# Reordering the expert stage of a two-layer transformer kernel

## The reference, cut to what matters

```python
xn = _layernorm(x, axis=-1)
x = x + _L1_attn_ref(xn, ...) + _L1_ffn_ref(xn, ...)

# _L1_attn_ref
scores = jnp.einsum('bhqd,bhkd->bhqk', q, k) * scale
scores = jnp.where(causal, scores, jnp.float32(-jnp.inf))
probs = jax.nn.softmax(scores, axis=-1)
attn = jnp.einsum('bhqk,bhkd->bhqd', probs, v)
out = attn @ weight_proj.T

# _L1_ffn_ref, E = 32, K = 4, CAP = 32
probs = jax.nn.softmax(x @ Wr, axis=-1)
topw, topi = jax.lax.top_k(probs, K)
topw = topw / jnp.sum(topw, axis=-1, keepdims=True)
shared = silu(x @ Wsg) * (x @ Wsu) @ Wsd
shared = shared * jax.nn.sigmoid(x @ Wse)
pos = (jnp.cumsum(oh, axis=0) * oh).sum(-1) - 1        # oh: one-hot of the chosen experts
xe = jnp.zeros((E, CAP, h), x.dtype).at[sel, posc].add(x[tok] * valid[:, None])
g = silu(jnp.einsum('ech,ehf->ecf', xe, Wg))
u = jnp.einsum('ech,ehf->ecf', xe, Wu)
ye = jnp.einsum('ecf,efh->ech', g * u, Wd)
out = shared.at[tok].add(ye[sel, posc] * (w * valid)[:, None])
```

## Time and profile before

| | |
|---|---|
| median of 3 runs | 461.1 us (460.25 to 461.37) |
| profiled execution | 461.18 us, span 459.2 us |
| TensorE matmul busy | 427.9 us (93%) |
| VectorE busy | 311.3 us (68%) |
| ScalarE busy | 245.5 us (53%) |
| GpSimd busy | 165.7 us (36%) |
| TensorE, 372.21 to 438.87 us | 54.23 us busy of 66.66, mean granted clock 0.92 |

### The profile page before, as it was taken

The page is one execution under the profiler, slowest core; times in us unless marked ns, Lnnn a source line. Parts: engine busy times, 40 slices in busy tenths (PEclk is TensorE's granted clock), DMA queues, the critical chain, the costliest instruction groups (busy, mean ns, idle before and its releaser), DMA issues.

```text
span 459.2 us, 8817 instructions
## 1 busy us (share of the span) xinstructions
PE 427.9 (93%) x3054; PEld 380.9 (83%) x3054; DVE 311.3 (68%) x901; ACT 245.5 (53%) x669; POOL 165.7 (36%) x293
## 2 busy tenths in 40 slices
PE   2999999999999999999999999999998889785997
PEld 1788888899999999999999999999976655564787
DVE  5645576678787878787877766586779636948142
ACT  3464561786868787868676873332254225502020
POOL 3050001545454555555555301021650061897000
PEclk9999999999999999999999999999999999988899
DMA  6820011401010101010000000001999039950002
GB/s 192 214 74 2 1 46 47 156 29 47 2 46 1 47 3 46 1 49 1 0 2 2 0 1 25 13 11 30 340 312 301 11 117 300 284 149 0 1 12 80
DMA packets 41978, 34.45 MB, mean 75 GB/s; under 512 B 6688, under 2 KB 40144, under 8 KB 41936
## 3 DMA queue, kind: packets, MB, share of 16 engines
q1 hardware_dynamic: 41552, 32.85, 25.1%
q0 software_dynamic: 384, 1.05, 0.7%
HBM read 31.80 MB, written 2.10 MB: 74 GB/s over the span
## 4 chain that ended last, share of the span: by engine, by line
PE 87%; DVE 8%; ACT 2%; issue 2%; DMA 1%; POOL 0%; DVEq 0%
PE bank L910 21%; PE bank L912 21%; PE bank L911 21%; PE bank L1068 4%; PE bank L1080 3%; PE bank L1059 3%; DVE GT L1752 2%; PE bank L1309 2%; PE bank L1310 2%; PE bank L1285 2%; PE bank L1110 2%; PE bank L1267 1%; DVE ACTl L1810 1%; DVE OS L1756 1%; PE bank L1298 1%
## 5 line engine op out<-in xcount | busy, mean ns | idle before, releaser
L573 POOL TENSOR_TENSOR arena<-arena,rinv 128x384 f32<-128x384 f32 x64 | 52.9, 827 | 82.2 <-DVE rinv L1550 82.2
L910 PE MATMUL bank<-XTl,WA 128*128 128x512 f32 x128 | 54.4, 425 | 2.6 <-POOL WA L540 1.7
L912 PE MATMUL bank<-XTh,WA 128*128 128x512 f32 x128 | 51.4, 401 | 0.0
L911 PE MATMUL bank<-XTh,WA 128*128 128x512 f32 x128 | 51.3, 401 | 0.0
L739 ACT ACTIVATE PT<-bank 128x256 fp32r<-128x256 f32 x64 | 24.4, 381 | 34.2 <-PE bank L1068 34.2
L1554 DVE TENSOR_TENSOR PT<-bank,PT 128x256 fp32r<-128x256 f32 x64 | 27.2, 425 | 19.7 <-ACT arena L740 19.7
L910 PE MATMUL bank<-WA,XTh 128*128 128x256 f32 x128 | 38.4, 300 | 0.6 <-DVE K L1525 0.6
L911 PE MATMUL bank<-WA,XTl 128*128 128x256 f32 x128 | 35.8, 279 | 0.0
L564 POOL CAST Q<-arena 128x128 fp32r<-128x128 f32 x64 | 18.6, 290 | 47.7 <-PE bank L912 47.6
L912 PE MATMUL bank<-WA,XTh 128*128 128x256 f32 x128 | 35.7, 279 | 0.0
L1542 DVE CUSTOM_DVE_ANT_0 arena<-bank,posm 128x128 f32<-128x128 f32 x64 | 18.1, 283 | 20.9 <-PE bank L912 20.9
(11 more groups left out here) (326 smaller groups left out, 1453.8 us busy)
## 6 DMA issues: line engine op xcount, KB each, us to landing
arena<-in_L_ffn_Wg SPq DMA_DIRECT2D x6, 704.0 KB, 7.8
arena<-in_L_ffn_Wu SPq DMA_DIRECT2D x6, 704.0 KB, 9.7
arena<-in_L_ffn_Wd SPq DMA_DIRECT2D x6, 512.0 KB, 8.1
arena<-in_L_attn_Wq SPq DMA_DIRECT2D x4, 512.0 KB, 6.5
arena<-in_L_attn_Wk SPq DMA_DIRECT2D x8, 256.0 KB, 2.6
arena<-in_L_attn_Wv SPq DMA_DIRECT2D x8, 256.0 KB, 3.3
arena<-in_L_attn_Wo SPq DMA_DIRECT2D x1, 2048.0 KB, 8.2
arena<-in_L_ffn_Wd SPq DMA_DIRECT2D x6, 192.0 KB, 7.5
```

Source lines behind the costliest of these rows:

```text
L573: pool.tensor_tensor(pr, pr, r[:, :, None].to_broadcast([P, 3, P]), ALU.mult).then_inc(s_p, 1)
L910: pe.matmul(dst, wh, xl, start=start, stop=False)
L911: pe.matmul(dst, wl, xh, start=False, stop=False)
L912: return pe.matmul(dst, wh, xh, start=False, stop=stop)
```

## The change

The list of steps is written anew. The step "parts" is taken apart into "weigh" (second softmax part), "split" (n = 0: the shared down weights; n = 1 to 6: one block of hidden values each), "mask" (two masks each), "high" and "low" (three high and low parts each) and "add" (a shared addition); these stand between the steps of the groups. slots(n) stands one group further ahead; slots(1) goes to bank 3 instead of bank 1. All twelve shared products come before slots(0). The small softmax is done for tiles 0 to 5 (384 of 512 elements) early, in the gate stage and at up(0), and for tiles 6 and 7 (128 elements) later; GpSimd walks the tiles in order 0 to 7 and waits for the second part at tile 6. In the gate stage shared_product(1) stands before the slot positions and g_low(2) before slots_of(0), slot_table(7) before shared_up(8, 0), and on VectorE the table's copy and two sums of scores before shared_product(8). slots(0) no longer waits for the slot weights, turn(0) does. The transposes of the attention output wait for the last expert output only before the fourth bank.

```diff
@@ -26,14 +26,16 @@
-EXPERT_STEPS = [("shared", (8, 1)), ("table", 0), ("shared", (9, 0)), ("shared", (9, 1)), ("shared", (10, 0)), ("shared", (10, 1)),
-                ("slots", 0), ("up", 0), ("shared", (11, 0)), ("shared", (11, 1)), ("slots", 1), ("up", 1), ("turn", 0),
-                ("slots", 2), ("down", 0), ("turn", 1), ("up", 2), ("down", 1), ("slots", 3), ("turn", 2), ("up", 3),
-                ("down", 2), ("turn", 3), ("slots", 4), ("down", 3), ("parts", 0), ("sd", 0), ("sd", 1),
-                ("up", 4), ("slots", 5), ("sd", 2), ("turn", 4), ("sd", 3), ("down", 4),
-                ("up", 5), ("slots", 6), ("sd", 4), ("turn", 5), ("sd", 5), ("down", 5),
-                ("up", 6), ("slots", 7), ("sd", 6), ("turn", 6), ("sd", 7), ("down", 6), ("mix", 0), ("mix", 1),
-                ("up", 7), ("mix", 2), ("turn", 7), ("mix", 3), ("down", 7)]
+EXPERT_STEPS = [("shared", (8, 1)), ("table", 0)]
+EXPERT_STEPS += [("shared", (q, k)) for q in (9, 10, 11) for k in range(2)]
+EXPERT_STEPS += [("slots", 0), ("slots", 1), ("up", 0), ("slots", 2), ("up", 1), ("turn", 0), ("slots", 3), ("up", 2),
+                 ("down", 0), ("turn", 1), ("slots", 4), ("up", 3), ("down", 1), ("turn", 2), ("down", 2), ("turn", 3), ("sd", 0),
+                 ("weigh", 0), ("split", 0), ("down", 3), ("split", 1), ("sd", 1), ("split", 2), ("split", 3),
+                 ("up", 4), ("slots", 5), ("split", 4), ("sd", 2), ("split", 5), ("turn", 4), ("split", 6), ("sd", 3),
+                 ("down", 4), ("mask", 0), ("up", 5), ("slots", 6), ("mask", 2), ("sd", 4), ("turn", 5), ("sd", 5), ("down", 5),
+                 ("mask", 4), ("high", 0), ("up", 6), ("slots", 7), ("high", 3), ("low", 0), ("sd", 6), ("turn", 6), ("mask", 6),
+                 ("sd", 7), ("low", 3), ("add", 7), ("down", 6), ("mix", 0), ("mix", 1), ("up", 7), ("mix", 2), ("turn", 7),
+                 ("mix", 3), ("down", 7)]
...
@@ -610,21 +618,20 @@
-            for f in range(2):
-                pool.wait_ge(s_ap, 1)
-                for i in range(4):
-                    j = 2 * i + f
...
+            for j in range(NT):
+                i, f = j // 2, j % 2
+                pool.wait_ge(s_ap, 1 + j // 6)
...
@@ -840,6 +847,8 @@
+            act.wait_ge(s_am, 1)
+            nc.scalar.activation(SCp[0], SCp[0], ACT.Exp, scale=SCALE1).then_inc(s_ae, 1)
             silu(3)
...
-                if what == "parts":
-                    act.wait_ge(s_am, 1)
-                    nc.scalar.activation(SCf, SCf, ACT.Exp, scale=SCALE1).then_inc(s_ae, 1)
+                if what == "weigh":
+                    act.wait_ge(s_am, 2)
+                    nc.scalar.activation(SCp[1], SCp[1], ACT.Exp, scale=SCALE1).then_inc(s_ae, 1)
+                if what == "split" and n == 0:
                     act.wait_ge(s_sd, 32)
                     act.wait_ge(s_ps, 2)
                     act.wait_ge(s_gl, FC)
                     nc.scalar.activation(SDh[:], SD, ACT.Copy).then_inc(s_sdh, 1)
+                if what == "split" and n >= 1:
                     act.wait_ge(s_sm, len(shared))
-                    for m in range(FC):
-                        nc.scalar.activation(ACTh[:, m], ACTT[m][:, N // 2:N], ACT.Copy).then_inc(s_adh, 1)
-                if what == "down" and n == 5:
-                    act.wait_ge(s_dn, 6)
-                    act.wait_ge(s_sw1, 1)
-                    for i in range(6):
+                    nc.scalar.activation(ACTh[:, n - 1], ACTT[n - 1][:, N // 2:N], ACT.Copy).then_inc(s_adh, 1)
+                if what == "high":
+                    if n == 0:
+                        act.wait_ge(s_dn, 6)
+                        act.wait_ge(s_sw1, 1)
+                    for i in range(n, n + 3):
                         y_high(i)
...
@@ -1234,8 +1245,8 @@
             slot_table(6)
+            slot_table(7)
             shared_up(8, 0)
-            slot_table(7)
...
                 if g == 0:
-                    pe.wait_ge(s_sw1, 1)
                     pe.wait_ge(s_sm, 9)
+                elif g == 1:
+                    pe.wait_ge(s_sm, 10)
                 else:
-                    pe.wait_ge(s_xe, g)
+                    pe.wait_ge(s_xe, 1 if g == 2 else g)
...
                 pe.wait_ge(s_eh, g + 1)
-                if g >= 1:
+                if g == 0:
+                    pe.wait_ge(s_sw1, 1)
+                else:
                     pe.wait_ge(s_ec, g)
...
-            pe.wait_ge(s_ye, GR)
             pe.wait_ge(s_pv, 32)
             for f in range(4):
+                if f == 3:
+                    pe.wait_ge(s_ye, GR)
...
+            def scores_less_max(part):
+                step(nc.vector.tensor_reduce(MXp[part], SCp[part], AX, ALU.max))
+                nc.vector.tensor_tensor(SCp[part], SCp[part], MXp[part][:, :, :, None].to_broadcast([P, 2, (3 - 2 * part) * H1, 4]),
+                                        ALU.subtract).then_inc(s_am, 1)
+
+            def scores_weighed(part):
+                dve.wait_ge(s_ae, part + 1)
+                step(nc.vector.tensor_reduce(MXp[part], SCp[part], AX, ALU.add))
+                step(nc.vector.reciprocal(MXp[part], MXp[part]))
+                nc.vector.tensor_tensor(SCp[part], SCp[part], MXp[part][:, :, :, None].to_broadcast([P, 2, (3 - 2 * part) * H1, 4]),
+                                        ALU.mult).then_inc(s_ap, 1)
+
             shared_product(0)
+            dve.wait_ge(s_sr, 6)
+            scores_less_max(0)
             dve.wait_ge(s_qc, NT)
             top_k(NT - 2)
...
+            shared_product(1)
             dve.wait_ge(s_po, 1)
...
+            g_low(2)
             slots_of(0)
-            g_low(2)
-            shared_product(1)
             shared_product(2)
...
             shared_product(7)
             slots_of(7)
+            sum_products(6)
+            dve.wait_ge(s_di, NT)
+            nc.vector.tensor_copy(TK[0:TC, 512:1024], pb[5][0:TC]).then_inc(s_tkd, 1)
+            sum_products(7)
+            g_low(5)
...
                 ins.then_inc(s_ix, 1)
+                shared_product(8)
...
                 if what == "table":
-                    dve.wait_ge(s_di, NT)
-                    nc.vector.tensor_copy(TK[0:TC, 512:1024], pb[5][0:TC]).then_inc(s_tkd, 1)
-                    g_low(5)
                     slot_weights()
+                    sum_products(8)
+                    dve.wait_ge(s_sr, 9)
+                    scores_less_max(1)
...
+                if what == "up" and n == 0:
+                    scores_weighed(0)
+                if what == "split" and n == 0:
                     dve.wait_ge(s_sdh, 1)
                     nc.vector.tensor_tensor(SDl[:], SD, SDh[:].bitcast(F32), ALU.subtract).then_inc(s_sdl, 1)
...
+                if what == "split" and n == 3:
+                    scores_weighed(1)
+                if what == "mask":
+                    if n == 0:
+                        dve.wait_ge(s_it, 4)
+                    slot_mask(n)
+                    slot_mask(n + 1)
+                if what == "low":
+                    for g in range(n, n + 3):
+                        y_low(g)
                 if what == "sd" and n >= 1:
                     add_shared(n - 1)
-                if what == "mix" and n == 0:
-                    add_shared(NT - 1)
+                if what == "add":
+                    add_shared(n)
```

More of the change, by code:

```diff
@@ L211, in program @@
         SC = region(30720, 512).rearrange("p (f i h j) -> p f i h j", f=2, i=4, h=H1)
-        SCf = region(30720, 512).rearrange("p (x j) -> p x j", j=4)
+        SCr = region(30720, 512).rearrange("p (f x j) -> p f x j", f=2, j=4)
+        SCp = [SCr[:, :, 0:3 * H1], SCr[:, :, 3 * H1:4 * H1]]
         XN2 = region(31744, 2048).rearrange("p (j n) -> p j n", j=NT)
@@ L238, in program @@
         sig = sb("sig", [P, NT])
-        mx1 = sb("mx1", [P, 128])
+        mx1 = sb("mx1", [P, 2, 4 * H1])
+        MXp = [mx1[:, :, 0:3 * H1], mx1[:, :, 3 * H1:4 * H1]]
         pvt = sb("pvt", [P, 256])
@@ L405, in down_bank, with slots_bank @@
             return (0, 2, 3)[j % 3]
+        def slots_bank(g):
+            return 3 if g == 1 else 1
         def up_bank(q):
@@ L612, in _ @@
             chain = 0
[L613 to L621 removed]
+            for j in range(NT):
+                i, f = j // 2, j % 2
+                pool.wait_ge(s_ap, 1 + j // 6)
+                for k in range(i + 1):
+                    v = QS[:, 2 * k + f, 0:QKV].rearrange("p (g n) -> p g n", g=G1)[:, :, None, GW - D1:GW].to_broadcast([P, G1, 4, D1])
+                    p = SC[:, f, i, :, k].rearrange("p (g r) -> p g r", g=G1)[:, :, :, None].to_broadcast([P, G1, 4, D1])
+                    dst = AO[:, j] if k == 0 else pvt[:]
+                    pool.tensor_tensor(dst.rearrange("p (g r d) -> p g r d", g=G1, r=4), p, v, ALU.mult).then_inc(s_pv, 1)
+                    chain += 1
+                    pool.wait_ge(s_pv, chain)
+                    if k:
```

(41 more changed lines are left out.)

13 lines of the change are left out of this document (2 added, 11 removed).

## The result

The changed kernel took 443.7 us (median of four runs, 443.37 to 444.25) against 461.11 us for the kernel before on the same chip: a ratio of 0.9627, with a 95% interval of 0.961 to 0.9644. The forecast was 443.3 us. The profiled execution took 443.39 us, with a span of 441.4 us.

What follows compares the result with a forecast made beforehand. TensorE, 87% of the chain, bounds the kernel through waits and low clock. Front 1.9, up(1) 0.96, small waits 0.25, queue 9.5, clock 3.6, transposes 0.5, overhangs 1.1: 17.8 us off 461.18 gives 443.4 (median 443.3); range 441.5 to 445.

Steps and rivals of the forecast that it cites:

- The front: Gate and slot table stage: the turn of the slot table comes at 365.05 instead of 366.98 us, 1.9 us earlier.
- The gathers: Gathers ahead of the expert stage: cost 0 to 0.6 us, taken as 0, by the idle queue's 2.6 us landing.
- slots a group ahead: Early expert stage on TensorE: 0.96 us before up(1) goes, and small waits of 0.30 us shrink by 0.25 us.
- VectorE's queue: Expert stage: TensorE's waits of 2.62, 1.34, 5.11 and 0.94 us go, less 0.5 us that stay: 9.5 us.
- mix(0): End of the expert stage: mix(0) starts at 412.7 us, TensorE arriving at 412.2 and waiting 0.5 us.
- The clock: TensorE's low-clock stretches after the long waits (0.64 for 4.70 us, 0.51 for 4.40 us) go: 3.6 us.
- the overhangs: TensorE: each vanished wait takes the overhang of the matmul before it, about 0.16 us for seven, 1.1 us.
- Rival (d): Expert stage, 372 to 383 us: short steps with waits bring the granted clock down for good; slower, up to 477; chance 0.03.
- Rival (a): Last stretch before mix(0): VectorE bounds it, GpSimd ends after 415, some 3 us wait and lower clock; 447.5 us; chance 0.2.
- Rival (b): Front gives nothing: the moved table step costs what it saves and a gather is late; 445.2 us; chance 0.12.
- Rival (c): ScalarE's table switch ahead of the exp costs a second pause, delaying VectorE's chain; 444.0 us; chance 0.04.
- Rival (e): Expert stage: weights arrive late, so the order does not do what it says; gain vanishes if landing after 433; chance 0.03.

Runs made afterwards that it cites:

- the second experiment: The changed kernel with slot_table(7) put back behind shared_up(8,0), all else as changed: 442.07 us, ratio 0.9569 to the kernel before.

## Why the prediction was right

**Waits and work.** The sum can be checked as a whole. On TensorE the waits from 341 us on were 16.4 us before and are 3.9 after, so 12.5 us of the 17.8 are waits, and the other 5.3 are TensorE's shorter busy time. The forecast had 13.1 us of waits (1.9, 0.96, 0.25, 9.5 and 0.5) and 4.7 of clock and overhangs. Each half was right in kind and off by 0.6 us, one up and one down. That the median was hit within 0.4 us and the span to the tenth is in part luck.

**The front (1.9 us forecast, 2.13 measured at the turn).** The product went where it should, and the experiment that put it back brought the wait back. The wait of 1.5 us before slot_table(7) came as forecast, 1.52. What the forecast did not say is that this part of the change is an error: it took the move as the price of the copy's, and the second experiment shows that the turn is just as early without it. The first small softmax took 0.54 and 0.91 us rather than two steps of 0.5, and what follows on VectorE came 0.33 us late; the positions' matmuls covered it, as said.

**The gathers (forecast free).** The first went out at 366.72 us (forecast 366.9); landing took:

```profile
DMA to landing us min/median/max: 2.7/3.6/6.6
```

The rows answer to the earlier trace rows. No turn of the gathered rows waited, so the value chosen, of an idle queue, held.

**slots a group ahead (0.96 and 0.25).** The mechanism is right, and the waits went; the trace without it puts it at 0.8 us in place of 1.2, because part of what is won there only arrives earlier at mix(0). In the forecast each wait was a gain of its own.

**VectorE's queue (9.5).** Right within 0.35 us at turn(4) and turn(5), with two errors against each other: `SDl` took 2.18 us, not 1.65, since it stood beside GpSimd (1.76 in the two kernels in which GpSimd was idle there), and the first five parts took 0.8 to 0.9 us each where the forecast had 1.06. The small lots of parts and of masks each carry weight, and they don't add up: undone singly they cost 3.4 and 2.9 us, and each time the wait before mix(0) vanished in return.

**mix(0) (0.5 forecast, 1.13 measured).** This term was mis-sized most. The forecast had one mask beside GpSimd; there were two and the first low part, as GpSimd's last step ends at 408.1:

```profile
407.02 1.08 POOL L632 TENSOR_TENSOR arena<-arena,pvt 128x256 f32<-128x256 f32 x1
```

VectorE let mix(0) go 0.2 us later than forecast, and TensorE got there 0.4 us sooner (411.8, not 412.2). Only the 0.2 us count for the time; TensorE's earlier arrival gains nothing. The sign that the forecast named, no idle time over 1 us from 373 us on, is missed by 0.13 us.

**The clock (3.6) and the overhangs (1.1).** The granted clock stood at 1.00 from 372 to 441 us, and the two terms together stand against the 5.3 us less of busy time. The overhangs were not tested alone. For the clock there is a check: the forecast has 1.7 us for the stretch at 0.64, and where one such stretch came back, behind GpSimd's late start and behind the lump of parts, 1.5 and 1.8 us were lost beside the wait. In the kernel with masks in lumps, whose trace kept its clock, 0.3 us were (2.9 us of span, 2.6 of waits). Rival (d), the short steps that bring the clock down, did not come about.

**Rival (a)** was right as a mechanism and wrong for this kernel: it takes GpSimd's late start, and then gives 446.99 where I had 447.5. **Rival (b)** fell: the front gave more than its term. But half of its premise holds: the moved table step did cost 1.5 us and, by the second experiment, saved nothing. **Rival (c)** fell by this stretch of ScalarE:

```profile
383.50 0.26 ACT L890 ACTIVATE arena<-bank 48x128 f32<-48x128 f32 x1
383.78 1.28 ACT L893 ACT_TABLE_LOAD   x1
385.07 0.31 ACT L893 ACTIVATE arena<-arena 128x128 f32<-128x128 f32 x1
```

The load starts when the copy ends and the exp when the load ends, as in the earlier trace rows. The Trainium skill ("ScalarE: Activation LUTs", "What ACT_TABLE_LOAD costs") states 1.38 us of draining beside the load. Neither trace has room for it, and the measurement decides. **Rival (e)** fell: the last issue of the weights is at 401.00, against 401.77 in the earlier trace rows, and no up or down waited for its weights.

## What to carry to other kernels

When an engine with much to do feeds one that is never to wait, split its lumps and put each lot behind the step that is needed first, then walk its queue to the single point that nothing can be put behind; that point (mix(0) here) swallows part of what is won ahead of it, so single gains don't add up. A helper engine off the chain can still set its length, as instructions of the busy engine take longer beside it: start it early, even if its result is needed late. And ask of each step in a change whether it is needed for the gain: here one of them cost 1.5 us and was hidden in a result of 17 us.

## What the runs showed of the hardware

**Idle time and the granted clock.** The same idle time did and did not bring the clock down. After 2.62 us of idleness the mean over the next few us was 0.64 in the kernel before and 1.00 in the trace with masks in lumps; after 2.69 us it was 0.58, after 2.94 us 0.59, after 5.11 us 0.51, and waits of 1.57 us and less never lowered it in these traces. It is not the order of the work alone that decides. The very same kernel went both ways: with masks in lumps two executions of four had a mean clock of 1.000 and two of 0.996, with GpSimd late one had 1.000 and three had 0.992 to 0.996. So a forecast should carry both outcomes for a wait of 2.6 to 2.9 us, with some 1.5 to 1.8 us between them. What decides in the single case was not tried.

**GpSimd and VectorE.** While `SDl` ran for 2.18 us (1.75 in the earlier trace rows), a step of GpSimd that takes 0.73 us next to it took 2.13:

```profile
385.90 0.73 POOL L632 TENSOR_TENSOR arena<-arena,pvt 128x256 f32<-128x256 f32 x1
...
387.43 2.13 POOL L632 TENSOR_TENSOR arena<-arena,pvt 128x256 f32<-128x256 f32 x1
```

Each engine's instructions take longer beside the other's: a part took 0.69 us without GpSimd at work and up to 1.13 beside it, two masks 1.41 and up to 2.37. This agrees with the Trainium skill ("SBUF — State Buffer", "SBUF: two separate sides"), which has the two engines lock one port pair in turn. That parts beside GpSimd took 0.82 to 0.88 us at some places and 1.13 at others I had not expected, and why is left open.
